# Two cross-attention layers: fewer semaphore waits on TensorE, halved key projections, int8 weight steps by piece, column exponentials behind bank copies

## What is computed

```python
x = x + L0_xattn(ctx, ctx, layernorm(x), mask)          # masked, 1024 keys
x = x + L0_attn(layernorm(x), ...)                      # linear attention
x = x + L0_ffn(layernorm(x), clip_x, clip_down, w_gate, w_up, w_down)   # int8 fake quantisation
x = x + L1_xattn(layernorm(x), ctx, ctx, ...)           # unmasked
x = x + L1_attn(layernorm(x), Wq, Wk, Wv, W_O)          # causal
x = x + L1_ffn(layernorm(x), w_gate, w_up, w_down)      # fp4, blocks of 16

def _weight_fake_quant(w):                              # of L0_ffn
    scale = max(abs(w), axis=1, keepdims=True) / 127.0
    return clip(round(w / scale), -128.0, 127.0) * scale
```

## Time and profile before

| | us |
|---|---|
| median of three runs (1373.24 to 1374.25) | 1373.98 |
| the profiled execution | 1370.36 |
| its span, first to last instruction | 1368.3 |
| first layer's loop of 64 steps, from its first scores | 29.5 to about 517 |
| second layer's loop of 64 steps | 732 to about 1257 |

### The profile page before, as it was taken

How to read it: one execution, slowest core, us unless ns; L and a number is a source line. 1 busy time by engine, 2 the same in 40 slices (tenths; PEclk the granted TensorE clock), 3 DMA queues, 4 the chain that set the end, 5 groups by cost and what they waited for, 6 DMA issues and landing times. The chain is left out here.

```text
span 1368.3 us, 32530 instructions
## 1 busy us (share of the span) xinstructions
PE 1229.0 (90%) x12656; PEld 887.8 (65%) x12658; DVE 951.4 (70%) x1543; ACT 857.8 (63%) x1373; POOL 660.1 (48%) x897
## 2 busy tenths in 40 slices
PE   6999999999999988897978999998889998988886
PEld 3666767676777765554645667676667676766654
DVE  3787886787777773684676776676756677756674
ACT  3766767667777754543546667676768676767331
POOL 1665555455565642340013446355654657746533
PEclk9999999999999999999999999999999999999998
DMA  4311322111112203001633021002001132000000
GB/s 157 100 55 55 124 61 77 55 56 55 55 56 85 95 2 115 1 1 31 200 115 88 32 63 54 32 33 63 32 33 54 45 81 64 32 2 2 5 9 19
DMA packets 32853, 78.49 MB, mean 57 GB/s; under 512 B 4416, under 2 KB 16448, under 8 KB 28480
## 3 DMA queue, kind: packets, MB, share of 16 engines
q1 hardware_dynamic: 32704, 76.42, 18.2%
HBM read 69.07 MB, written 7.34 MB: 56 GB/s over the span
## 5 line engine op out<-in xcount | busy, mean ns | idle before, releaser
L697 POOL TENSOR_TENSOR ca_fold<-ca_probT 128x512 f32<-128x512 f32 x128 | 164.0, 1281 | 235.9 <-ACT ca_probT L927 235.4
L936 ACT ACTIVATE ca_probT<-bank 128x512 f32<-128x512 f32 x256 | 140.2, 595 | 110.8 <-PE bank L830 109.5
L801 PE MATMUL bank<-ca_kT,ca_q_blk 32*128 32x512 f32 x512 | 146.4, 648 | 9.7 <-DVE ca_probT L1016 7.1
L830 PE MATMUL bank<-ident,ca_prob 128*128 128x128 f32 x1024 | 144.5, 282 | 11.0 <-DVE ca_picked L1028 5.3
L807 PE MATMUL bank<-ca_q_blk,ca_kT 32*128 32x128 f32 x2048 | 150.9, 286 | 0.0
L927 ACT ACTIVATE ca_probT<-ca_probT 128x1024 f32<-128x1024 f32 x128 | 135.5, 1059 | 18.1 <-DVE ca_probT L1016 12.1
L739 PE MATMUL bank<-ca_ctxT,ca_wk 128*128 128x512 f32 x256 | 123.1, 606 | 9.1 <-DMA ca_bk<-in_L_xattn_bk 9.1
L847 PEld LDWEIGHTS bank<-ca_probT,ca_v 128*32 128x32 f32 x4096 | 109.8, 111 | 32.6 <-issue 26.7
L755 PE MATMUL bank<-wv,ctxT 128*128 128x256 f32 x512 | 129.6, 382 | 1.1 <-ACT fw_upT L383 0.6
L830 PEld LDWEIGHTS bank<-ident,ca_prob 128*128 128x128 f32 x1024 | 109.8, 141 | 31.2 <-DVE ca_picked L1028 7.2
L847 PE MATMUL bank<-ca_probT,ca_v 128*32 128x128 f32 x4096 | 126.9, 276 | 3.3 <-issue 1.8
(11 more groups left out here) (324 smaller groups left out, 2606.1 us busy)
## 6 DMA issues: line engine op xcount, KB each, us to landing
ca_ctxT<-in_ctxT SPq DMA_DIRECT2D x16, 1024.0 KB, 5.2
ctxT<-in_ctxT SPq DMA_DIRECT2D x16, 1024.0 KB, 4.7
ca_mask_i<-in_mask SPq DMA_DIRECT2D x32, 256.0 KB, 6.3
ek_ctxT<-in_ctxT SPq DMA_DIRECT2D x12, 512.0 KB, 5.6
early_k<-ek_out SPq DMA_DIRECT2D x48, 128.0 KB, 3.5
ca_kT<-early_k SPq DMA_DIRECT2D x12, 512.0 KB, 5.8
ca_mask_col_i<-in_mask_keys SPq DMA_DIRECT2D x16, 256.0 KB, 6.4
lat<-in_x SPq DMA_DIRECT2D x1, 1024.0 KB, 4.9
```

Source lines behind the costliest of these rows:

```text
L697: pool.tensor_tensor(f[:, :, :], p[:, 0:4, :], p[:, 4:8, :], ALU.add).then_inc(self.fold_step, 1)
L801: mm = pe.matmul(self.core.bank[:, 2 + half, :], self.q_blk[rows, b % 2, u, :, :], self.kT[rows, b % 2, u, :], start=True, stop=True, tile ...
L830: tr = pe.transpose(self.core.bank[:, x, n * P:(n + 1) * P], self.prob[:, s % 2, (4 * h + n) * P:(4 * h + n + 1) * P], self.core.ident[:, :])
L936: self.banks.free(act.activation(self.probT[:, n % 2, 4 * h:4 * h + 4, 2 * (s % 2) + 1, :], self.core.bank[:, x, :].rearrange("p (n q) -> ...
```

## The change

- TensorE's waits: several waits are left out where one engine's order covers them: for the scores one of two or three, for the product with the values one ("t", the last transposes' copy) in place of up to ten; the turn no longer waits for its bank, and the spread waits once for it. In the second layer the wait for the subtraction (`below_ready`) stands behind the row scores.
- First layer: the first half of the key projection goes ahead of the turn, the second stays behind it.
- ScalarE: the column exponentials go behind the weight copies and the query copy of the step, in the second layer behind the causal block's copies too.
- int8 weights: VectorE rounds one piece a step, GpSimd subtracts it (`whole_on_pool`) ahead of that step's `spread_rows`, and transposes and copies come three steps later.

```diff
@@ -393,7 +393,7 @@
     ROWS = [P] * (IC - 1) + [I_LAST]
     UNITS = 3
-    STEPS = 5
+    STEPS = 2 + IC
...
         elif n == 1:
             dve.wait_ge(self.step, 3 * x + 1)
             dve.tensor_scalar(scale, self.mag[:, 0:pieces], 1.0 / QMAX, None, ALU.mult).then_inc(self.step, 1)
-        elif n == 2:
             dve.wait_ge(self.step, 3 * x + 2)
             dve.reciprocal(self.inv[:, 0:pieces], scale).then_inc(self.step, 1)
-        elif n == 3:
-            dve.wait_ge(self.step, 3 * x + 3)
-            for c in range(pieces):
-                dve.tensor_scalar(raw[:, c, :], raw[:, c, :], self.inv[:, c:c + 1], ROUND, ALU.mult, ALU.add)\
-                    .then_inc(self.rounded, 1)
-        else:
-            if x >= 1:
-                self.banks.wait_filled(dve, ("i", x - 1, self.UNITS - 1))
-            for c in range(pieces):
-                dve.wait_ge(self.rounded, first + c + 1)
-                dve.tensor_scalar(whole[:, c, :], raw[:, c, :], ROUND, None, ALU.subtract).then_inc(self.ready, 1)
+        elif n - 2 < pieces:
+            c = n - 2
+            if c == 0:
+                dve.wait_ge(self.step, 3 * x + 3)
+            dve.tensor_scalar(raw[:, c, :], raw[:, c, :], self.inv[:, c:c + 1], ROUND, ALU.mult, ALU.add)\
+                .then_inc(self.rounded, 1)
+
+    def whole_on_pool(self, pool, x, c):
+
+        pieces, width = (IC, D) if x < 2 else (KD, FF)
+        if c < pieces:
+            if c == 0 and x >= 1:
+                self.banks.wait_filled(pool, ("i", x - 1, self.UNITS - 1))
+            pool.wait_ge(self.rounded, x * IC + c + 1)
+            pool.tensor_scalar(self.whole[:, c * width:(c + 1) * width], self.raw[:, c * width:(c + 1) * width], ROUND,
+                               None, ALU.subtract).then_inc(self.ready, 1)
...
-    def open(self, pe, key, bank=None):
+    def open(self, pe, key, bank=None, known_free=False):
...
-        wait(pe, self.taken[bank], self.count[bank])
+        if not known_free:
+            wait(pe, self.taken[bank], self.count[bank])
...
         if u % 2 == 0 and b not in self.early_batches:
-            for half in range(2):
-                self.banks.wait_taken(pe, ("k", 4 * b + u + half))
+            self.banks.wait_taken(pe, ("k", 4 * b + u + 1))
         if s >= 1:
-            if self.masked:
-                pe.wait_ge(self.masked_ready, s)
-                pe.wait_ge(self.max_ready, s)
-            else:
-                pe.wait_ge(self.below_ready, s)
-                pe.wait_ge(self.exp_done, s)
+            pe.wait_ge(self.max_ready if self.masked else self.exp_done, s)
...
         mm.then_inc(self.row_scores, 1)
+        if s >= 1 and not self.masked:
+            pe.wait_ge(self.below_ready, s)
         for c in range(4):
...
-        x = self.banks.open(pe, ("turned", s), 4)
+        x = self.banks.open(pe, ("turned", s), 4, known_free=True)
...
     def spread_top(self, pe, s):
 
-        self.banks.wait_taken(pe, ("turned", s))
         x = self.banks.open(pe, ("spread", s), 4)
...
-    def transposes(self, pe, s):
-
-        pe.wait_ge(self.exp_done, s + 1)
-        for h in range(2):
+    def transposes(self, pe, s, halves=range(2)):
+
+        if self.masked or s == STEPS - 1:
+            pe.wait_ge(self.exp_done, s + 1)
+        for h in halves:
...
     def times_v(self, pe, n):
...
-        for s in self.step_of_values(n):
-            for h in range(2):
-                self.banks.wait_taken(pe, ("t", s, h))
-        for i in range(4):
-            self.banks.wait_taken(pe, ("v", 4 * b + i))
-        pe.wait_ge(self.column_exp, 2 * n + 2)
+        last = ("t", 2 * n + 1, 1)
         x = self.banks.open(pe, ("pv", n))
+        if self.banks.at[last][0] != x:
+            self.banks.wait_taken(pe, last)
...
         pe.wait_ge(self.column_sum_ready, 2 * n + 2)
-        pe.wait_ge(self.row_sum_ready, 2 * n + 2)
...
@@ -1090,15 +1087,17 @@
                     ca.project_v(pe, s + 2)
+                if s + 4 < STEPS:
+                    ca.project_k(pe, s + 4, parts=(0,))
                 if s < STEPS:
                     ca.turn_column_max(pe, s)
                 if s + 4 < STEPS:
-                    ca.project_k(pe, s + 4)
+                    ca.project_k(pe, s + 4, parts=(1,))
                 if s < STEPS:
                     ca.spread_top(pe, s)
                 for x in range(3):
-                    if 6 <= s - IW_STEPS[x] < 9:
-                        ffn_weights.transposes_on_tensor(pe, x, s - IW_STEPS[x] - 6)
+                    if 9 <= s - IW_STEPS[x] < 12:
+                        ffn_weights.transposes_on_tensor(pe, x, s - IW_STEPS[x] - 9)
...
+                for x in range(3):
+                    if 2 <= s - IW_STEPS[x] < ffn_weights.STEPS:
+                        ffn_weights.whole_on_pool(pool, x, s - IW_STEPS[x] - 2)
                 if s < STEPS:
                     ca.spread_rows(pool, s)
                     ca.add_columns(pool, s)
...
                     ca.take_k(act, s + 4)
-                if s < STEPS:
-                    ca.column_exponentials(act, s)
                 if s == STEPS:
                     early.take(act, END_PIECES[0], END_BANKS)
                 for x in range(3):
-                    if 6 <= s - IW_STEPS[x] < 9:
-                        ffn_weights.take_on_scalar(act, x, s - IW_STEPS[x] - 6)
+                    if 9 <= s - IW_STEPS[x] < 12:
+                        ffn_weights.take_on_scalar(act, x, s - IW_STEPS[x] - 9)
                 if s == Q_STEPS[0]:
                     ca.take_q_on_scalar(act, 1)
+                if s < STEPS:
+                    ca.column_exponentials(act, s)
...
@@ -2526,19 +2528,19 @@
-                ca.column_exponentials(act, s)
                 for x in range(3):
                     if s in FW_TRANSPOSE[x]:
                         weights.take_on_scalar(act, x, FW_TRANSPOSE[x].index(s))
                 if s == Q_STEPS[0]:
                     ca.take_q_on_scalar(act, 1)
+                for t in tile_at(s, 7):
+                    sa.take_transposed(act, t)
+                ca.column_exponentials(act, s)
...
-                for t in tile_at(s, 7):
-                    sa.take_transposed(act, t)
```

More of the change, by code:

```diff
@@ L433, in step_on_vector @@
         raw = self.raw[:, 0:pieces * width].rearrange("p (c n) -> p c n", n=width)
-        whole = self.whole[:, 0:pieces * width].rearrange("p (c n) -> p c n", n=width)
         if n == 0:
```

## The result

The changed kernel takes 1335.99 us (median of four runs, 1335.32 to 1337.36); the kernel before took 1373.61 in the same comparison. The ratio is 0.9734, 95% interval 0.9717 to 0.975: 37.6 us less, where 30.3 were forecast and 1334 to 1358 was the range: the result lies 2.0 inside its lower end. The profiled execution took 1335.32 us, its span is 1333.5, the granted clock 0.98 of full speed, as before.

The account below looks back on a forecast made before the run. TensorE's order was taken as the bound. First layer 20.8 + 6.4 - 4.2 = 23.0, second 7.3 (terms 8.45): 30.3 off the profiled 1370.36, plus 3.6 to the median, gave 1343.7, say 1343; range 1334 to 1358 us.

Parts of the forecast that it names:

- ScalarE's order: Second layer: causal block's copies ahead of the column exponentials end four waits of L830, some 0.65 us each, 2.6 in all.
- subtraction's wait behind row scores: Second layer: where that wait is late, column scores end when they ended before; nothing taken, a gain of 2 as bound.
- five L755 waits: First layer: value projections waiting for a bank, two for `take_pv`, three for weight copies; removing them gains 6.4 us.
- Key halves around the turn: First layer: half the key projection ahead of L814 fills its waits, gaining 0.37 in step 44; sum 20.8 us, from below 10.
- Where TensorE is behind its inputs, extra waits cost nothing: TensorE's surplus waits cost only where it has just been released; the forecast counted their removal in the second layer alone.
- Spread's doubled wait: Second layer: L821 starts 0.15 after L998's end where 0.06 is possible; 0.09 x 46 waits, 4.1 us.
- Product's waits: Second layer: L847 follows the spread by 0.55 in one of five "issue" cases; 5 x 0.35, 1.75 us.
- Rounding and GpSimd: First layer's added costs: VectorE's roundings 1.6 us, two beside GpSimd's mask conversion 1.4; GpSimd's subtraction nothing on the path.
- Rival 1: First layer's gain half comes through: odd steps keep nothing, even steps half, weight copies cost 0.66 each; 1356 us, chance 0.18.
- Rival 2: VectorE and GpSimd block each other over 14 roundings and 14 subtractions, 26.9 us on the path; 1370 us, chance 0.04.
- Rival 3: Second layer: row and column scores stop running beside each other, up to 1.1 us a step; 1412 us, chance 0.03.
- Rival 4: First layer: the stall only moves from L814 to L821, because VectorE sets the tops; 1366 us, chance 0.04.

## Why the prediction was right, step by step

The sum was right, its terms were not all. The chain of kernels adds the parts one by one; each number is the worth of a part with those above it in place, the first loop's in steps 4 to 61, the second's with the clock's part off:

| part | first loop, forecast | measured | second loop, forecast | measured |
|---|---|---|---|---|
| fewer waits, alone | 0 | 0.7 | 4.1 + 1.75 | 3.7 |
| key halves, with them | 20.8 | 15.6 | | |
| ScalarE's order, int8 in bursts | 2.6 | 4.9 | 2.6 | 4.6 |
| int8 by piece, with the above | 2.6 - 3.0 | 2.1 | | |
| subtraction's wait behind row scores | | | 0 | 0.5 |
| step 62 of the first layer; clock of the second | | -0.1 | | 1.7 |
| sum | 23.0 | 23.2 | 7.3 (8.45 added) | 10.5 |

(Of the five L755 waits, 6.4, three stand here with ScalarE's order, 3.8, less the 1.2 of odd steps, and two with the pieces, 2.6. The second loop's 4.6 is what is left of the chain's 5.1 without the subtraction's 0.5; undoing ScalarE's order alone cost 4.2.)

That 23.2 met 23.0 is luck: the halves came out 5.2 under their term, and ScalarE's order 2.3, the pieces 2.5 and the waits 0.7 over theirs.

- **Key halves around the turn, 20.8.** Mechanism right (0.37 and 0.15 came out as 0.34 to 0.40 and 0.16 or 0.22); the size was off: 15.6, or 12.9 with all else in place. It took every idle time ahead of L814 for the halves. Of the 11.1 us of waits, 1.9 is a single one in step 62, where no keys are projected and a half can't fill it; here are the waits of the kernel before from 500.4 us on:

```profile
PE bank L814 <- DVE ca_column_max L976: 1.9, 1, 1.9
```

Those behind bursts have two remedies. In step 9, which became 2.01 shorter, the halves do with bursts what they do without, and the pieces with whole keys lose only 0.16 of it; in step 8 (1.71) the pieces alone give 1.28, the halves with bursts 0.50. So part of the pieces' worth was counted here.
- **"Where TensorE is behind its inputs, extra waits cost nothing: L847 follows L821 by 0.20 with all of them".** This is the step that failed, as used for the first layer. It was read off a kernel in which the spread came late, and the change takes just that lateness away. Once the halves are there, all the waits cost 8.1 in the first loop, and putting back the product's alone costs 4.8: more than in the second layer, to which the forecast gave all their worth. The time doesn't show the error, since the change makes both edits.
- **Spread's doubled wait, 0.09 x 46 = 4.1:** 0.15 became 0.06 as forecast, in sum 2.9; not all 46 lay on the path. **Product's waits, 5 x 0.35:** 0.8.
- **ScalarE's order.** Each case is worth 1.02 to 1.09, where 0.65 was taken for the second layer. With the pieces' timing there are six such cases in the first layer, not three: 6.6 there. The forecast charged odd steps with a weight copy 0.2 each; the kernel with the old order shows no change over 0.08 in them.
- **Rounding and GpSimd.** One of fourteen roundings took 1.23 where 0.35 is usual, beside the mask conversion; two at 0.7 more were counted. GpSimd's subtraction takes 0.85 and 1.97 (estimated 0.7 and 1.9), and nothing waits for it.

Rival 1 (half comes through) was wrong for the change and near in size for the halves alone (8.3 of 20.8), for another reason: it let odd steps keep nothing and even ones half, and odd steps keep all and even ones a quarter, because of the product's waits. Rival 2 fell: the change took 1336.0, not 1370, and with both instructions on VectorE the loop is longer, not shorter. By the Trainium skill, SBUF — State Buffer, Who interferes with whom, all 28 instructions might have blocked the other engine; in the trace one rounding is long, and one of GpSimd's mask conversions, begun 0.06 behind a rounding, took 2.93 where 2.77 is usual. Rival 3 fell: the two kinds of scores start 0.01 to 0.06 apart except in the four steps where the wait is late. Rival 4 fell: L820's waits are 4.2 (below 5, as asked), 0.9 more than the spread's before.

## What to carry to other kernels

Before a wait or an instruction in an engine's order is called free because something else is late there, ask whether the same change makes that something early: here the surplus waits and the late spread hid each other, and either cure alone gave 0.7 or 8.3 of the 16.4 that both gave. So an edit that measures as nothing isn't refuted until the other half of its pair is in. When the total agrees with a forecast, the terms still may not; a chain of kernels from the old to the new, one part at a time from both ends, shows it at the price of a few runs. And with engines this evenly loaded, what frees a bank (a copy, a division) goes ahead of what only feeds the slower chain.

## What was not expected of the hardware

Waits on TensorE that had all long been met still take time when they are queued behind one that has not. From the end of the tops on VectorE to the start of the next product it is 0.31 us with one wait for the spread and one or two for the product, 0.37 with two more for bank 4, 0.58 with up to ten for the product, 0.70 with both. These are the least values of either loop, and both loops have the same to 0.01. The Trainium skill, TensorE: Matmul & The Clock Gate, Step-by-step: what each phase is for, says that weight loads are pulled ahead in a window 64 deep; by that alone the product would follow the spread at once. The 0.20 agrees while TensorE is behind its inputs; the 0.46 and 0.55 do not once it has been released, and here the measurement decides. The number of wait instructions is what counts, 0.106 for each whether it reads one semaphore or two, as the four and five of them above show.

The clock stretch above wasn't expected either: in the five kernels with the subtraction's wait ahead of the row scores TensorE ran at 1.2 GHz for some 3.4 us in this step each time (there it had idled 1.85 for the wait), in the eight with the wait behind them (idle for 0.81 there) in two, after records and waits that are the same to a hundredth in those with and without. So one profile of a kernel is worth no more than 1.6 us here, and whether the moved wait makes the dip rarer, and is worth more than its 0.5, isn't settled.
